# Layer 0's routing and most of its scatter in the cross attention, expert weights resident, shared expert and norm beside the gathers

## The reference

```python
# cross attention: 8 heads of 128, keys of both batches together (154)
sim = q @ k.T * SCALE; sim = (sim - mean) * 1.5 + mean
out = softmax(sim) @ v @ Wout + bout
# feed forward: 32 experts, 4 for each token, at most C rows in an expert
scores = sigmoid(X @ gate_w.T)
_, idx = top_k(scores + bias, 4)
w = scores[idx] / sum(scores[idx])
pos = place of this (token, choice) among those of its expert, in token order
xe[expert, pos] = X[token]                # where pos < C (C = 256 here)
h = silu(xe @ W1) * (xe @ W3);  ye = h @ W2
out = sum over 4 choices of w * ye[expert, pos]   # nothing where pos >= C
out = out + silu(X @ sw1.T) * (X @ sw3.T) @ sw2.T # the shared expert
```

## Time and profile before

| | us |
|---|---|
| median of 3 runs (3815.13 to 3822.75) | 3821.08 |
| the profiled execution | 3814.49 |
| its span | 3812.7 |
| PE / DVE / ACT / POOL busy in the span | 2785.7 / 1749.8 / 1253.3 / 789.5 |

### The profile page before, as it was taken

How to read it: one execution, slowest core, us unless ns; L and a number is a source line. 1 busy time by engine, 2 the same in 40 slices (tenths; PEclk the granted TensorE clock), 3 DMA queues, 4 the chain that set the end, 5 groups by cost and what they waited for, 6 DMA issues and landing times. The chain is left out here.

```text
span 3812.7 us, 42749 instructions
## 1 busy us (share of the span) xinstructions
PE 2785.7 (73%) x15498; PEld 1586.8 (42%) x15498; DVE 1749.8 (46%) x3825; ACT 1253.3 (33%) x2524; POOL 789.5 (21%) x648
## 2 busy tenths in 40 slices
PE   7799995785340768887875779697576788768786
PEld 3333334564230323333353266374443233346575
DVE  4566645333354555555523458243322676533412
ACT  3234441331120135555621400222213244435421
POOL 0101110122544346666620200001001000001100
PEclk9889997996685879999987879796698799879898
DMA  2311102301265232222211200200001311030032
GB/s 95 86 32 36 37 2 71 116 1 36 79 196 81 70 83 40 40 34 33 28 13 55 39 9 17 97 3 26 12 1 60 43 24 25 2 93 1 17 123 67
DMA packets 175663, 183.06 MB, mean 48 GB/s; under 512 B 53086, under 2 KB 141744, under 8 KB 174692
## 3 DMA queue, kind: packets, MB, share of 16 engines
q1 hardware_dynamic: 162979, 166.83, 15.4%
q0 software_dynamic: 12480, 13.57, 3.9%
HBM read 121.81 MB, written 61.59 MB: 48 GB/s over the span
## 5 line engine op out<-in xcount | busy, mean ns | idle before, releaser
L834 POOL TENSOR_TENSOR l1a_p_lo<-res,l1a_p_hi 128x1024 f16<-128x1024 f32 x144 | 266.6, 1852 | 209.9 <-ACT res L1032 209.7
L1055 DVE TENSOR_REDUCE l1a_nmax<-ps 128x1 f32<-128x512 f32 (+3 forms) x384 | 200.3, 551 | 147.3 <-PE ps L889 116.6
L1055 DVE TENSOR_REDUCE l0a_nmax<-ps 128x1 f32<-128x512 f32 (+3 forms) x384 | 200.9, 555 | 122.4 <-PE ps L889 93.4
L1055 DVE TENSOR_REDUCE l3a_nmax<-ps 128x1 f32<-128x512 f32 (+3 forms) x384 | 199.3, 553 | 80.2 <-PE ps L889 65.5
L1039 ACT ACTIVATE l0a_probs<-ps 128x1024 f32<-128x1024 f32 (+1 forms) x192 | 145.7, 811 | 229.9 <-PE ps L917 182.3
L1031 ACT ACTIVATE l1a_p_hi<-ps 128x1024 f16<-128x1024 f32 x192 | 158.0, 823 | 158.6 <-PE ps L917 132.9
L1039 ACT ACTIVATE l3a_probs<-ps 128x1024 f32<-128x1024 f32 (+1 forms) x192 | 148.6, 809 | 184.0 <-PE ps L917 147.6
L886 PE MATMUL ps<-l1a_ks,l1a_qs 128*128 128x512 f16 (+3 forms) x384 | 124.7, 345 | 95.4 <-DVE l1a_nmax L1055 74.3
L914 PE MATMUL ps<-l1a_qs,l1a_ks 128*128 128x512 f16 (+3 forms) x768 | 167.6, 333 | 22.4 <-ACT res L1032 22.4
L889 PE MATMUL ps<-mask,ident_b 128*128 128x128 bf16 x768 | 171.8, 231 | 0.0
L886 PE MATMUL ps<-l3a_ks,l3a_qs 126*128 126x512 f16 (+3 forms) x384 | 126.7, 354 | 44.8 <-DVE l3a_nmax L1055 20.0
(11 more groups left out here) (661 smaller groups left out, 6359.2 us busy)
## 6 DMA issues: line engine op xcount, KB each, us to landing
f_w<-in_L_ffn_w_dram SPq DMA_DIRECT2D x16, 1024.0 KB, 7.4
f_slots<-x0a_zeros SPq DMA_DIRECT2D x32, 256.0 KB, 7.2
f_xe<-f_slots SPq DMA_DIRECT2D x32, 256.0 KB, 3.7
f_ys<-f_y SPq DMA_DIRECT2D x32, 256.0 KB, 3.1
l1a_qs<-l_q_h SPq DMA_DIRECT2D x64, 128.0 KB
f_wf<-in_L_ffn_W_dram SPq DMA_DIRECT2D x96, 64.0 KB, 2.8
l0a_qs<-l_q_h SPq DMA_DIRECT2D x32, 128.0 KB
l0a_ks<-l_k_h SPq DMA_DIRECT2D x16, 256.0 KB
```

What stands on the lines that cost most here:

```text
L834: pool.tensor_tensor(ph_lo[:, n % SLOTS, :, 0:w], probs[:, n % FULL, :, 0:w], ph_hi[:, n % SLOTS, :, 0:w], ALU.subtract).then_inc(s_["low_ ...
L1055: dve.tensor_reduce(nmax[:, s % LEAD, f.chunk, f.p, f.tile:f.tile + f.n], src, AX.X, ALU.max, negate=True).then_inc(s_["maxed"], 1)
```

## The change

1. The router becomes a class `Router` that works on one group of four tiles at a time, inside the turns of the cross attention. `choose` and `number` are the old instructions of VectorE on a quarter of the tiles; `score` is the sigmoid. Counts of earlier groups are carried in `upto`. Its PSUM banks are those of the columns, so the columns of a group wait for `routed` of the group before.
2. `Routes` holds what outlives the phases: `acc`, `gates`, `flat`, `tops`, `to_slot`, `of_slot`, the semaphores `wall_ld` and `scattered`, and `wall`, the weights of all 32 experts and the shared one (loaded once, by three transfers, during the cross attention; the host's layout gives 1536 bytes a partition and expert in one piece).
3. GpSimd issues the 16 scatters of group 0 in turns 9 to 11, those of group 1 in turns 13 to 15, those of group 2 after its loop. Only group 3's stay in the expert phase. The wait for the cleared slots moves from SP to GpSimd ahead of the first scatter.
4. In the expert phase the shared expert of groups 0 and 1 is computed ahead of the experts (two groups side by side), that of 2 and 3 behind them, beside the gathers. SP issues no weights.
5. The phase of the norm goes. VectorE normalizes a group after its 16 additions, in the same program.

```diff
+class Router:
+    def logits_of(self, pe, g):
+        pe.wait_ge(self.s["prepared"], 6)
+        pe.wait_ge(self.s["xts_ready"], g + 1)
+        if g:
+            pe.wait_ge(self.s["routed"], g)
+        for j in range(GT):
+            t = g * GT + j
+            for d in range(DC):
+                ins = pe.matmul(self.logits[:, j, :], k.xtr[:, d, t * P:(t + 1) * P], self.wg[:, d, :], start=d == 0, stop=d == DC - 1)
+        ins.then_inc(self.s["logits_done"], 1)
+    def places_of(self, pe, g):
+        pe.wait_ge(self.s["mask_ready"], g + 1)
+        for j in range(GT):
+            pe.matmul(self.place[:, j, :], self.before[:], self.mask[:, j, :], start=True, stop=False)
+            ins = pe.matmul(self.place[:, j, :], self.ones[:], self.earlier[:, j, :], start=False, stop=True)
+        ins.then_inc(self.s["placed"], 1)
+    def score(self, act, g):
...
+    def choose(self, dve, g):
+        ch = self.chain = self.chain or Count(dve, self.s["route_chain"], 0, 0)
+        sel, gt, eq, rank, mask, by_expert = self.sel, self.gt, self.eq, self.rank, self.mask, self.by_expert
+        dve.wait_ge(self.s["prepared"], 6)
+        dve.wait_ge(self.s["sc_ready"], g + 1)
+        ch.step(dve.tensor_tensor(sel[:], self.sc[:], self.bias[:, None, :].to_broadcast([P, GT, E0]), ALU.add))
+        ch.wait()
+        for j in range(GT):
+            ch.step(dve.max(self.m8[:, j, :], sel[:, j, :]))
+        ch.wait()
+        least = self.m8[:, :, K0 - 1:K0].to_broadcast([P, GT, E0])
+        ch.step(dve.tensor_tensor(gt[:], sel[:], least, ALU.is_gt))
+        ch.step(dve.tensor_tensor(eq[:], sel[:], least, ALU.is_equal))
+        ch.wait()
+        ch.step(dve.tensor_reduce(self.need[:], gt[:], AX.X, ALU.add))
+        ch.step(dve.tensor_tensor_scan(rank[:].rearrange("p t e -> p (t e)"), self.reset[:].rearrange("p t e -> p (t e)"),
+                                       eq[:].rearrange("p t e -> p (t e)"), 0.0, ALU.mult, ALU.add))
+        ch.wait()
+        ch.step(dve.tensor_scalar(self.need[:], self.need[:], -1.0, float(K0), ALU.mult, ALU.add))
+        ch.wait()
+        ch.step(dve.tensor_tensor(rank[:], rank[:], self.need[:, :, None].to_broadcast([P, GT, E0]), ALU.is_le))
+        ch.wait()
+        ch.step(dve.tensor_tensor(eq[:], eq[:], rank[:], ALU.mult))
+        ch.wait()
+        ch.step(dve.tensor_tensor(mask[:], gt[:], eq[:], ALU.add))
+        ch.wait()
+        ch.step(dve.tensor_copy(by_expert[:], mask[:].rearrange("p t e -> p e t")))
+        ch.step(dve.tensor_tensor(self.share[:], self.sc[:], mask[:], ALU.mult))
+        ch.wait()
+        if g:
+            ch.step(dve.tensor_tensor(by_expert[:, :, 0], by_expert[:, :, 0], self.upto[:, (g - 1) % 2, :, GT - 1], ALU.add))
+            ch.wait()
+        ch.step(dve.tensor_tensor_scan(self.upto[:, g % 2].rearrange("p e t -> p (e t)"), self.resets[:].rearrange("p e t -> p (e t)"),
+                                       by_expert[:].rearrange("p e t -> p (e t)"), 0.0, ALU.mult, ALU.add))
+        ch.wait()
+        dve.tensor_tensor(self.earlier[:], self.upto[:, g % 2].rearrange("p e t -> p t e"), mask[:], ALU.subtract).then_inc(self.s["mask_ready"], 1)
+        ch.step(dve.tensor_reduce(self.total[:], self.share[:], AX.X, ALU.add))
+        ch.wait()
+        ch.step(dve.tensor_scalar(self.total[:], self.total[:], 1e-12, None, ALU.max))
+        ch.wait()
+        ch.step(dve.reciprocal(self.inv[:], self.total[:]))
+        ch.wait()
+        ch.step(dve.tensor_tensor(self.share[:], self.share[:], self.inv[:, :, None].to_broadcast([P, GT, E0]), ALU.mult))
+        ch.wait()
+    def number(self, dve, g):
+        keep = self.keep
+        rows = slice(g * GT, (g + 1) * GT)
+        ch = self.chain
+        dve.wait_ge(self.s["placed"], g + 1)
+        ch.step(dve.scalar_tensor_tensor(out=self.kept[:], in0=self.place, scalar=float(CAP0), in1=self.mask[:], op0=ALU.is_lt, op1=ALU.mult))
+        ch.step(dve.tensor_tensor(self.earlier[:], self.place, self.slot[:, None, :].to_broadcast([P, GT, E0]), ALU.add))
+        ch.wait()
+        ch.step(dve.tensor_tensor(keep.flat[:, rows, :], self.earlier[:], self.kept[:], ALU.mult))
+        ch.step(dve.tensor_tensor(keep.gates[:, rows, :], self.share[:], self.kept[:], ALU.mult))
+        ch.wait()
+        for t in range(g * GT, (g + 1) * GT):
+            ch.step(dve.max(keep.tops[:, t, :], keep.flat[:, t, :]))
+        ch.wait()
+        top = keep.tops[:, rows, 0:K0]
+        ch.step(dve.tensor_scalar(self.miss[:], top, 0.0, float(SLOTS0 + 1), ALU.is_equal, ALU.mult))
+        ch.step(dve.tensor_scalar(keep.of_slot[:, rows, :], top, -1.0, 0.0, ALU.add, ALU.max))
+        ch.wait()
+        dve.scalar_tensor_tensor(out=keep.to_slot[:, rows, :], in0=top, scalar=-1.0, in1=self.miss[:], op0=ALU.add, op1=ALU.add).then_inc(self.s["routed"], 1)
 def cross_rows(...):
             def _(sp):
...
+                    for e in range(0, E0 + 1, 11):
+                        sp.dma_start(keep.wall[:, e:e + 11, :], k.a["L0_ffn_W"][e:e + 11].rearrange("e p f -> p e f")).then_inc(keep.s["wall_ld"], 16)
             def _(pool):
...
+                    if router and t == 2 * GT:
+                        pool.wait_ge(s_["cleared"], 16 * (SLOTS0 // (2 * P)))
+                    if router and t > 2 * GT and t % GT:
+                        g = t // GT - 2
+                        if t % GT == 1:
+                            pool.wait_ge(s_["routed"], g + 1)
+                        for i in {1: range(0, 6), 2: range(6, 11), 3: range(11, 16)}[t % GT]:
+                            keep.scatter(pool, g * GT + i // K0, i % K0)
+                if router:
+                    pool.wait_ge(s_["routed"], NG - 1)
+                    for i in range(GT * K0):
+                        keep.scatter(pool, (NG - 2) * GT + i // K0, i % K0)
             def _(pe):
+                    if router and n >= 2 * GT - 1 and n % GT == GT - 1:
+                        router.logits_of(pe, n // GT - 1)
+                    if router and n >= 2 * GT and n % GT == 0:
+                        router.places_of(pe, n // GT - 2)
...
                 columns(NG - 1)
+                if router:
+                    router.logits_of(pe, NG - 1)
+                    router.places_of(pe, NG - 1)
             def _(dve):
+                    if router and n >= 2 * GT - 1 and n % GT == GT - 1:
+                        router.choose(dve, n // GT - 1)
+                    if router and n >= 2 * GT and n % GT == 0:
+                        router.number(dve, n // GT - 2)
                 normal(NG - 1)
+                if router:
+                    router.choose(dve, NG - 1)
+                    router.number(dve, NG - 1)
-def l0_gates(k, gates, flat, tops, to_slot, of_slot, xt_all):
...
 def routed_experts(...):
             def _(sp):
-                for e in range(LD):
-                    weights(e)
-                sp.wait_ge(s_["scattered"], 16 * NT * K)
+                sp.wait_ge(route.s["scattered"], 16 * NT * K)
...
                     if e + LD < E:
                         rows(e + LD)
-                        weights(e + LD)
             def _(pool):
-                for t in range(NT):
-                    for j in range(K):
-                        pool.indirect_dma_start(k.slots, ...)
+                for i in range(GT * K):
+                    route.scatter(pool, (NG - 1) * GT + i // K, i % K)
             def _(dve):
+                shared(0)
+                weights()
                 for i in range(E + 3):
...
+                shared(2)
...
+                    if (i + 1) % (GT * K):
+                        continue
+                    g = t // GT
+                    b = g % 2
+                    group = slice(g * GT, (g + 1) * GT)
+                    dve.wait_ge(s_["added"], i + 1)
+                    if g >= 2:
+                        dve.wait_ge(s_["xn_ready"], g - 1)
+                    dve.tensor_tensor(r[:, b], acc[:, group, :], k.xr[:, group, :], ALU.add).then_inc(s_["r_done"], 1)
+                    dve.wait_ge(s_["r_done"], g + 1)
+                    for q in range(GT):
+                        ch.step(dve.bn_stats(stats[:, b, q, :], r[:, b, q, :]))
+                    ch.wait()
+                    for q in range(GT):
+                        ch.step(dve.bn_aggr(mv[:, b, q, :], stats[:, b, q, :]))
+                    ch.wait()
+                    dve.tensor_scalar(ve[:, b, :], mv[:, b, :, 1], EPS, None, ALU.add).then_inc(s_["ve_ready"], 1)
+                    dve.wait_ge(s_["sd_ready"], g + 1)
+                    ch.step(dve.reciprocal(rs[:, b, :], sd[:, b, :]))
+                    ch.wait()
+                    for q in range(GT):
+                        ins = dve.tensor_scalar(k.xr[:, g * GT + q, :], r[:, b, q, :], mv[:, b, q, 0:1], rs[:, b, q:q + 1], ALU.subtract, ALU.mult)
+                    ins.then_inc(s_["xn_ready"], 1)
-        l0_gates(k, gates, flat, tops, to_slot, of_slot, k.xtr)
```

(25 more changed lines are left out.)

291 lines of the change are left out of this document (134 added, 157 removed).

## The result

| | before | after |
|---|---|---|
| median, us | 3818.11 (4 runs, 3813.98 to 3822.75) | 3724.93 (4 runs, 3708.89 to 3731.28) |
| the profiled execution / its span | 3814.49 / 3812.7 | 3708.89 / 3707.1 |
| first maximum of the cross attention to the last one | 169.3 | 185.5 |
| first maximum to the first read of the experts' rows | 326.3 | 263.0 |
| first read to first gather | 94.7 | 80.1 |

The ratio is 0.9749, 95% interval 0.9713 to 0.9786, 93.2 us by the medians. The forecast was 3716, in a range from 3703 to 3734, so the measured 3725 lies inside, 9 us above the point. The two profiles differ by 105.6 us. Of these 94.8 lie between the first maximum and the last copy, 1.0 is lost again in the phase change behind it, and the other 11.8 lie in stages that are the same code in both.

A forecast was written before the change was run, and what follows sets the result against it. No engine was full over the span; scatters and gathers paced by GpSimd and a router without overlap stood out. 73.0 + 17.1 - 2.5 + 17.6 = 105.2 off 3814.49 gives 3709.3, with 6.6 a median of 3716, range 3703 to 3734.

The forecast's parts named there:

- first term: Stages up to the first read of the experts' rows: that read at 943.9 for 1016.94, a gain of 73.0 us.
- 3.6 us a group, the logits included: Cross attention loop: routing delays the output matmuls from 782.46 to 786.1, for each of groups 0 and 1, 7.2 for two.
- Rival 4: Routing in the cross attention costs more: choose nearer 11 us, or the clock falls, 6.5 us a mask; 3736; chance 0.09.
- Rival 3: VectorE's work holds GpSimd in full: 39 us in GpSimd's chain for the 6.0 taken, 3749 us; chance 0.05.
- The steps at the loop's end: After the last tile: `routed` reaches 3 at 896.3, 16 scatters to 918.4, group 3's routing hidden by 2.7 us.
- the phase change took 1.76 us: Into the expert phase: 1.76 us from VectorE's last instruction to the first scatter, taken from before, giving 920.2.
- The experts' term: Expert loop without weight transfers: 26 turns at 2.11 us each, 54.8 for 71.9, a gain of 17.1 us.
- Rival 1: Experts stay bound by the transfers or their latency at 2.5 us or more: 3726 to 3733; chance 0.14.
- Rival 2: Experts run at the computing's 1.74 us a turn: 3706; chance 0.09.
- The gathers: Gathers behind the experts, beside shared expert and norms: only stretching, a loss of 2.5 us, bounds 0 and 12.
- the norm: Last addition to ScalarE's last copy: 8.4 us for 26.0, three groups lying beside gathers; a gain of 17.6 us.
- Rivals 5 and 6: 5: scatters between normalizations wait, slower than before, chance 0.01; 6: they push the cross attention out, 41 us lost, chance 0.02.

The follow-up runs named there:

- the second: The changed kernel profiled once more, nothing edited: loop 187.6 us for 185.5, last copy at 448.4 for 444.4, median 3730.2 us, ratio to before 0.9743.

## Why the prediction was right, and where it was off

Its first term, 73.0 us up to the first read, came out as 63.3. **The step that failed is "3.6 us a group, the logits included"**: it is 8.1 in both groups, 9.0 more for the two together. Two things are in the difference. (1) GpSimd's bias addition, due in the turns of tiles 8 and 12, holds VectorE's instruction with two inputs in SBUF: 6.4 us of the loop, shown by the run that moves it. The prediction had looked for this lock only the other way round. The Trainium skill, "SBUF — State Buffer", section "SBUF: two separate sides", gives the pair of ports to whichever of the two starts first. The trace agrees in group 0, with 2.33 us for 0.27 where GpSimd was first by 0.16 us; in group 1 VectorE's record starts 0.65 us before that of the addition and VectorE waits all the same, which the order of starts does not explain. (2) The step behind the one with choose, for which the sum had nothing: with the bias additions early the steps with choose are 3.2 and 3.9 us over, as forecast, and the two behind them 1.4 each, 2.8 in all. Their granted clock is 0.87 and 0.86: TensorE has waited 1.5 and 1.75 us for the mask and is at its low clock for a part of the step. Rival 4 named this fall, at 6.5 us a mask; it was far less. With choose in two parts and the numbering in a gap (2) goes too: group 0's four steps are 1.9 us over, the logits included, less than the 3.6.

Rival 3 had GpSimd wait for VectorE in full, 3749 us; that did not come: 16 scatters beside the shared expert took 22.6 us with the read's start, where I had 23.7.

The steps at the loop's end held: 28.9 us from the last maximum to the first scatter of group 2, where I had 29.1 (896.3 - 867.2); 20.4 for the 16 scatters, where I had 22.1; group 3's routing hidden by 1.9 us, where I had 2.7. **The second failure is "the phase change took 1.76 us"**: 5.56 behind the last scatter. I took the row of a phase that ended without a transfer of GpSimd in flight. So the 9.7 us missing from the first term are 9.0 and 3.8 too little, less 3.0 us of small terms that came out shorter than forecast (0.2, 1.7 and 1.1); that part is luck.

The experts' term was 17.1 and came to 14.6. The mechanism was right, a loop of read and store over six buffers, and the size a little off: 2.235 us a turn for 2.11 (3.3 us over 26 turns, of which 0.7 came back in the filling). I had taken the spacing of turns 3 to 6; that the stores of rows, which had hardly begun there, make the difference is likely and not shown. Rival 1 (bound by the transfers) fell by the run with eight buffers. Rival 2's 1.74 came with that run.

The gathers cost 0.8 us for the 2.5 forecast in the first profile (3.5 in the second), and the norm gave 17.7 for 17.6. Not in the sum was 1.0 us for the phase's end behind the norm (1.70 for 0.71). Together: 105.2 - 9.7 - 2.5 + 1.7 + 0.1 - 1.0 = 93.8.

Rivals 5 and 6 fell with the run that took all scatters out of the loop.

## What to carry to other kernels

Before work is put into an engine's idle time, take that time turn by turn, and count what already stands in the same turn (here a maximum, a copy, a normalization): what exceeds it delays everything behind it, and costs again through TensorE's clock. Look on both engines of the VectorE and GpSimd pair for long instructions with inputs in SBUF that would run beside the new work; to move one by some turns cost nothing and was worth 6.4 us of the loop, 4.8 at the first read. And when a queue is relieved, ask whether a count of buffers is the next bound: two more buffers gave 12 us here, nearly as much as the 13.5 of keeping 6 MB of weights resident.

## What the runs showed of the hardware

- A GpSimd addition of 128x1024 (2.35 us) held a VectorE instruction with two SBUF inputs until its end: 2.33 us for 0.27 where GpSimd's record starts first; in group 1 3.18 for 0.29, though VectorE's record starts 0.65 us earlier. With the additions moved both were short again.
- To leave a phase at whose end GpSimd still scatters took 5.56 us from the last scatter to the next one, in all eleven profiles with such an end; without them 1.6 to 1.8 us from VectorE's end.
- The DMA queue moved 284 to 286 GB/s at 89% busy in 1 and 1.5 KB pieces, and 238 GB/s at 78% with six buffers and no weights.
- Two profiles of one program differ by 4 us over 444, nearly all of it in how long TensorE stays at 1.2 GHz after a wait (8 output matmuls in 2.49 us in one and 3.75 in the other) and in the gathers (94.1 and 96.7).
